# A vision-transformer layer with a routed feed-forward on one core: routing weights spread by DMA, and the instruction orders of four engines rewritten

## The reference, cut to what matters

```python
h = tok(x)                                   # 16 images, 36 patches each: 576 tokens of 192
h = layernorm(h + attn(h))                   # 12 heads of 64, softmax over 36 keys
logits = h @ Wr + br                         # 8 experts
vals, idx = top_k(logits, 2); score = softmax(vals)
gu = h @ Wgu[e] + bgu[e]                     # for every expert e: 2 x 192 columns
gate = min(gu[:192], 7); up = clip(gu[192:], -7, 7)
down_e = ((up + 1) * gate * sigmoid(1.702 * gate)) @ Wd[e] + bd[e]
h = layernorm(h + sum over the 2 chosen e of score[e] * down_e)
```

## Time and profile before

| | us |
|---|---|
| median of 3 runs | 144.47 (144.03 to 145.9) |
| time of the profiled execution | 144.63 |
| its span, first to last instruction | 142.8 |
| PE busy | 132.8 (93%) |
| DVE busy | 101.1 (71%) |
| POOL busy | 79.5 (56%) |
| ACT busy | 76.0 (53%) |
| DMA queue q1, share of its 16 engines | 25.7% |

### The profile page before, as it was taken

How to read it: one execution, slowest core, us unless ns; L and a number is a source line. 1 busy time by engine, 2 the same in 40 slices (tenths; PEclk the granted TensorE clock), 3 DMA queues, 4 the chain that set the end, 5 groups by cost and what they waited for, 6 DMA issues and landing times. The chain is left out here.

```text
span 142.8 us, 4023 instructions
## 1 busy us (share of the span) xinstructions
PE 132.8 (93%) x1586; PEld 123.6 (87%) x1586; DVE 101.1 (71%) x255; ACT 76.0 (53%) x146; POOL 79.5 (56%) x92
## 2 busy tenths in 40 slices
PE   6999999999999999899999993999999999999950
PEld 2779899998989889899899973999999989999940
DVE  0129589468779598656786895478899786788752
ACT  3057889988933564868544481162422455433621
POOL 7303159670499999998640779166353254334511
PEclk9999999999999999999999997799999999999998
DMA  5999955720121225225810000000000000000021
GB/s 134 328 397 409 398 138 134 220 86 0 35 70 46 83 67 152 62 79 146 313 37 0 0 0 7 0 0 0 0 0 5 0 0 0 7 0 2 0 70 54
DMA packets 5962, 12.42 MB, mean 87 GB/s; under 512 B 888, under 2 KB 2872, under 8 KB 5944
## 3 DMA queue, kind: packets, MB, share of 16 engines
q1 hardware_dynamic: 5944, 12.18, 25.7%
HBM read 9.96 MB, written 0.44 MB: 73 GB/s over the span
## 5 line engine op out<-in xcount | busy, mean ns | idle before, releaser
L482 POOL TENSOR_TENSOR reg_r<-reg_p,reg_r 128x324 fp32r<-128x324 f32 (+1 forms) x23 | 19.0, 829 | 21.9 <-ACT reg_r L712 21.9
L408 POOL TENSOR_TENSOR reg_w<-stage,reg_w 128x768 fp32r<-128x768 f32 x12 | 22.5, 1887 | 6.8 <-ACT reg_w L544 6.7
L712 ACT ACTIVATE reg_r<-reg_p 128x324 fp32r<-128x324 f32 (+1 forms) x24 | 10.7, 444 | 27.6 <-DVE reg_p L1061 27.6
L1061 DVE SCALAR_TENSOR_TENSOR reg_p<-reg_q 128x324 f32<-128x324 f32 (+1 forms) x24 | 15.5, 645 | 2.2
L1038 DVE TENSOR_SCALAR reg_q<-ps,bup 128x324 f32<-128x324 f32 (+1 forms) x24 | 12.3, 511 | 6.7 <-PE ps L1283 6.5
L1279 PE MATMUL ps<-reg_r,reg_w 128*128 128x324 f32 (+1 forms) x48 | 15.1, 315 | 0.0
L1280 PE MATMUL ps<-reg_r,reg_w 128*128 128x324 f32 (+1 forms) x48 | 14.5, 302 | 0.0
L1281 PE MATMUL ps<-reg_r,reg_w 128*128 128x324 f32 (+1 forms) x48 | 14.5, 302 | 0.0
L1282 PE MATMUL ps<-reg_r,reg_w 128*128 128x324 f32 (+1 forms) x48 | 14.4, 300 | 0.0
L1283 PE MATMUL ps<-reg_r,reg_w 128*128 128x324 f32 (+1 forms) x48 | 14.3, 299 | 0.0
L703 ACT ACTIVATE reg_q<-ps,sm 128x324 f32<-128x324 f32 (+1 forms) x24 | 11.7, 489 | 3.3 <-PE ps L1283 3.3
(11 more groups left out here) (196 smaller groups left out, 393.5 us busy)
## 6 DMA issues: line engine op xcount, KB each, us to landing
reg_x<-xw_in SPq DMA_DIRECT2D x5, 416.0 KB, 6.1
stage<-w_gu_a SPq DMA_DIRECT2D x4, 384.0 KB, 4.5
stage<-w_gu_b SPq DMA_DIRECT2D x4, 384.0 KB, 3.4
reg_r<-reg_x SPq DMA_DIRECT2D x24, 54.0 KB
stage<-w_qkv_a SPq DMA_DIRECT2D x3, 384.0 KB, 7.7
stage<-w_qkv_b SPq DMA_DIRECT2D x3, 384.0 KB, 8.2
stage<-w_down SPq DMA_DIRECT2D x3, 384.0 KB, 4.0
wout<-w_out SPq DMA_DIRECT2D x1, 576.0 KB, 10.0
```

What stands on the lines that cost most here:

```text
L408: nc.gpsimd.tensor_tensor(dst[:, 1, :], raw, f(dst[:, 0, :]), ALU.subtract).then_inc(s_wlop, 1)
L482: nc.gpsimd.tensor_tensor(acts[:, n % NACT, 1, 0:w], act_f[:, n % 4, 0:w], f(acts[:, n % NACT, 0, 0:w]), ALU.subtract).then_inc(s_alo, 1)
L1061: nc.vector.scalar_tensor_tensor(out=act_f[:, n % 4, 0:w], in0=glu[:, n % 4, 0:w], scalar=GLU_LIMIT, in1=upw[:, n % 4, 0:w], op0=ALU.min, ...
```

## The change

- `spread(n)` leaves PE, and with it the one-hot matrix (and the small POOL and DVE instructions that build it). `choose` now sums its two picks and repeats the eight columns sixteen times, so that after `w_transpose` row p holds the score of expert p mod 8. A new ACT step `w_rows(b)` copies this to SBUF as wrow.
- SP issues 16 DMAs for each half that copy, for every unit, the row of its expert onto the unit's rows. They go from SBUF to SBUF, into the space of xs and V for the first half and into the stage buffers for the second. `weigh(n)` waits for these and reads its score from SBUF, no longer from PSUM.
- The lists of POOL, ACT, DVE and PE are reordered, as the diff shows.

Semaphore lists and the host's layout of bd are left out of the diff.

```diff
@@ -155,6 +154,9 @@
 
+        spread0 = reg_x[:, 0:NT * TS[0]].rearrange("p (c n) -> p c n", c=NT)
+        spread1 = stage[:, :, :].rearrange("p g n -> p (g n)")[:, 0:NT * TS[1]].rearrange("p (c n) -> p c n", c=NT)
+
@@ -350,6 +353,26 @@
                     sp.dma_start(wout[:, :, :], w_out).then_inc(s_wo, 16)
+            def spread(b):
+
+                sp.wait_ge(s_wrow, b + 1)
+                if b == 0:
+                    sp.wait_ge(s_pv, NU)
+                else:
+                    sp.wait_ge(*lo_done(16))
+                dst, cols = (spread0, spread1)[b], slice(TO[b], TO[b] + TS[b])
+
+                def rows(e, c, p0, n):
+                    src = wrow[p0 + e:p0 + n:E, cols].unsqueeze(1).to_broadcast([n // E, E, TS[b]])
+                    sp.dma_start(dst[p0:p0 + n, c, :], src).then_inc(s_spr[NT * b + c], 16)
+
+                for s in range(NPAIR):
+                    rows(2 * s, 3 * s, 0, 128)
+                    rows(2 * s + 1, 3 * s + 1, 0, 128)
+                    rows(2 * s, 3 * s + 2, 0, 64)
+                    rows(2 * s + 1, 3 * s + 2, 64, 64)
+            spread(0)
+            spread(1)
@@ -419,9 +442,6 @@
             nc.gpsimd.tensor_copy(pairs[:, ST:LANES], ident[:, SEQ:64]).then_inc(s_const, 1)
-            nc.gpsimd.tensor_tensor(rows2[:, :], ident[:, 0:2 * E], ident[:, 32:32 + 2 * E], ALU.add).then_inc(s_rows, 1)
-            pool.wait_ge(s_rows, 1)
-            nc.gpsimd.tensor_tensor(rows1[:, :], rows2[:, 0:E], rows2[:, E:2 * E], ALU.add).then_inc(s_rows, 1)
@@ -486,24 +506,25 @@
             for k in range(0, NU):
-                if k in (5, 6):
-                    root(k - 5, TSIZES[k - 5], s_ve, s_rstd)
-                if k in (3, 4, 5, 6):
-                    w_lo((7, 8, 9, 11)[k - 3])
+                if k in (3, 4, 5):
+                    w_lo(k + 4)
+                if k == 6:
+                    w_lo(10)
                 probs(k)
...
                     k_norm(k + 3)
-                if k == 5:
-                    w_lo(10)
+                if k in (4, 5):
+                    root(k - 4, TSIZES[k - 4], s_ve, s_rstd)
             root(2, TSIZES[2], s_ve, s_rstd)
+            w_lo(11)
+            gap_exp(0)
             w_lo(12)
-            gap_exp(0)
             gap_exp(1)
             gap_exp(2)
-            root(3, TSIZES[3], s_ve, s_rstd)
             w_lo(13)
...
             w_lo(15)
+            root(3, TSIZES[3], s_ve, s_rstd)
             act_lo(0)
@@ -512,9 +533,9 @@
             w_lo_tail(16)
+            gap_exp(3)
             act_lo(5)
             act_lo(6)
-            gap_exp(3)
             gap_exp(4)
@@ -685,6 +706,13 @@
                                      ACT.Copy).then_inc(s_h1hi, 1)
+
+            def w_rows(b):
+
+                first, last = W_BATCH[b][0], W_BATCH[b][-1]
+                o, n = TOFFS[first], TOFFS[last] + TSIZES[last] - TOFFS[first]
+                act.wait_ge(s_wt, last + 1)
+                nc.scalar.activation(wrow[:, o:o + n], ps[:, wt_bank(b), 0:n], ACT.Copy).then_inc(s_wrow, 1)
 
@@ -759,24 +787,25 @@
             pt_evac(7)
+            w_hi(13)
+            w_hi(14)
             o_evac(7)
             expert(0)
-            w_hi(13)
+            w_hi(15)
             expert(1)
+            w_hi(16)
+            w_rows(0)
             w2_hi(0)
...
             expert(3)
-            w_hi(14)
-            w_hi(15)
-            w_hi(16)
             act_hi(0)
...
             act_hi(3)
+            h1_evac(4)
             expert(5)
-            h1_evac(4)
             act_hi(4)
@@ -792,7 +821,8 @@
                 act_hi(n if n >= NT + 4 else n - 1)
-                if n == 11:
+                if n == 9:
+                    w_rows(1)
                     w2_hi(1)
@@ -817,9 +847,6 @@
             nc.vector.memset(tiny[:, :], TINY)
-            dve.wait_ge(s_rows, 2)
-            nc.vector.tensor_copy(onehot[:, :].rearrange("p (e n) -> p e n", e=E),
-                                  rows1[:, :].unsqueeze(2).to_broadcast([128, E, 128])).then_inc(s_onehot, 1)
@@ -1010,23 +1037,28 @@
                 rg = rt[:, g % 2]
-                iota = sm[0:n, C_IOTA:C_IOTA + 8].unsqueeze(1).to_broadcast([n, 3, 8])
+                iota = sm[0:n, C_IOTA:C_IOTA + 8]
                 dve.wait_ge(s_idx, g + 1)
                 dve.wait_ge(s_p2, g + 1)
+                if g >= 1:
+                    dve.wait_ge(s_w2, g)
+                for j in range(2):
+                    nc.vector.tensor_scalar(pick[0:n, j, :], iota, rg[0:n, j:j + 1], rg[0:n, 4 + j:5 + j],
+                                            ALU.is_equal, ALU.mult).then_inc(s_w1, 1)
+                dve.wait_ge(s_w1, 2 * g + 2)
                 if g >= 3:
                     dve.wait_ge(s_wt, g - 2)
-                for j in range(2):
-                    nc.vector.tensor_scalar(w2[0:n, g % 3, 0:96].rearrange("p (a e) -> p a e", a=3)[:, :, 8 * j:8 * j + 8],
-                                            iota, rg[0:n, j:j + 1], rg[0:n, 4 + j:5 + j], ALU.is_equal, ALU.mult)\
-                        .then_inc(s_w2, 1)
+                nc.vector.tensor_tensor(w2[0:n, g % 3, :].rearrange("p (a e) -> p a e", e=E),
+                                        pick[0:n, 0:1, :].to_broadcast([n, 16, E]), pick[0:n, 1:2, :].to_broadcast([n, 16, E]),
+                                        ALU.add).then_inc(s_w2, 1)
...
                 dve.wait_ge(s_w2hi, b + 1)
-                nc.vector.tensor_tensor(w2T[32:48, o:o + n], ps[32:48, wt_bank(b), 0:n],
-                                        f(w2T[32:48, o:o + n]), ALU.subtract).then_inc(s_w2lo, 1)
+                nc.vector.tensor_tensor(w2T[32:40, o:o + n], ps[32:40, wt_bank(b), 0:n],
+                                        f(w2T[32:40, o:o + n]), ALU.subtract).then_inc(s_w2lo, 1)
@@ -1040,11 +1072,12 @@
 
-                dve.wait_ge(s_bm, n + 1)
+                a, c = divmod(n, NT)
+                dve.wait_ge(s_spr[n], 32 if c % 3 == 2 else 16)
                 dve.wait_ge(s_u, n + 1)
-                w = TS[n // NT]
+                w = TS[a]
                 nc.vector.scalar_tensor_tensor(out=upw[:, n % 4, 0:w], in0=upw[:, n % 4, 0:w], scalar=1.0 - LIMIT,
-                                               in1=ps[:, B_BANK, 0:w], op0=ALU.max, op1=ALU.mult).then_inc(s_b, 1)
+                                               in1=(spread0, spread1)[a][:, c, :], op0=ALU.max, op1=ALU.mult).then_inc(s_b, 1)
 
@@ -1132,11 +1165,9 @@
             for k in range(2, NU):
-                if k in (5, 6):
-                    ln1_stats(k - 5)
-                row_sum(k)
                 if k == 5:
                     ln1(0)
+                row_sum(k)
                 if k + 1 < NU:
@@ -1144,6 +1175,8 @@
                     q_norm(k + 3)
+                if k in (4, 5):
+                    ln1_stats(k - 4)
             h1_lo(0)
@@ -1165,11 +1198,11 @@
             w2_lo(0)
+            up_in(2)
             ln1(3)
-            up_in(2)
+            h1_lo(3)
             weigh(0)
             expert_act(0)
-            h1_lo(3)
             weigh(1)
@@ -1181,24 +1214,26 @@
             up_in(5)
+            h1_lo(4)
             weigh(4)
             expert_act(4)
-            h1_lo(4)
+            read_logits(3)
+            rank(3)
             up_in(6)
...
             expert_act(5)
+            read_logits(4)
+            router_weights(3)
+            choose(3)
             up_in(7)
...
             expert_act(6)
-            read_logits(3)
-            rank(3)
-            read_logits(4)
+            rank(4)
             up_in(8)
...
             expert_act(7)
-            router_weights(3)
-            choose(3)
-            rank(4)
+            router_weights(4)
+            choose(4)
             for n in range(9, 2 * NT):
@@ -1209,10 +1244,7 @@
                     expert_in(n)
-                if n == 9:
-                    router_weights(4)
-                    choose(4)
-                if n == 11:
+                if n == 10:
                     w2_lo(1)
@@ -1512,26 +1544,6 @@
 
-            def spread(n):
-
-                a, c = divmod(n, NT)
-                s, k = divmod(c, 3)
-                if n == 0:
-                    pe.wait_ge(s_onehot, 1)
-                    pe.wait_ge(s_oev, NU)
-                    pe.wait_ge(s_w2lo, 1)
-                else:
-                    pe.wait_ge(s_b, n)
-                if n == NT:
-                    pe.wait_ge(s_w2lo, 2)
-                first = 256 * s + (0, 128, 64)[k]
-                mm(ps[:, B_BANK, 0:TS[a]], onehot[:, first:first + 128], w2T[:, TO[a]:TO[a] + TS[a]], start=True, stop=True)\
-                    .then_inc(s_bm, 1)
@@ -1599,10 +1611,10 @@
                     v_proj(4, (k - 2,))
+                if k in (4, 5):
+                    project(k - 4)
                 weighted(k - 2)
                 p_transpose(k - 1)
-                if k in (4, 5):
-                    project(k - 4)
             subtract_max(7)
@@ -1621,44 +1633,32 @@
             gate_up(2)
```

(27 more changed lines are left out.)

22 lines of the change are left out of this document (9 added, 13 removed).

## The result

The changed kernel takes 163.2 us (median of 4 runs, 162.12 to 165.48), the kernel before 145.17 beside it: a ratio of 1.1225, 95% interval 1.1084 to 1.1367. It is 12% slower, where I had forecast 3%. The profiled execution lasted 162.42 us, with a span of 160.6.

The account below looks back on a forecast made before the run. It took PE's matmuls to set the pace through the expert stage. Terms: -6.9 + 2.95 + 1.5 + 1.8 + 1.35 + 2.2 + 1.0 = +3.9, on 144.63 giving 148.5 us; range 143.0 to 151.5.

Parts of the forecast that it names:

- the part on h1_transpose(3): Before h1_transpose(3): three w_lo now precede root(3) on POOL, so PE stands 1.5 us (1.2 to 1.8).
- The spreads, -3.1: On PE: removing 24 spread matmuls, 12 x 0.143 + 12 x 0.115, takes 3.1 us off.
- The rest is work: Expert stage on PE: the old order loses about 3.7 us at down(0), and the rest is work.
- down(0), -2.47 and -1.3: At down(0): PE's stand of 2.47 us and 1.3 us of slow matmuls behind it go, 3.8 us gained.
- Attention, +2.95: In attention: PE stands at project(1) and exps(6) starts late on ACT, so project(2) loses 2.95 us (1.4 to 3.3).
- h1_transpose(4), +1.8: Now behind gate_up(4): PE stands 1.6 to 2.1 us for ln1(4), taken as 1.8.
- logits(3), +1.35: Now behind gate_up(5): PE waits 1.35 us (1.1 to 1.5) for h1_lo(4), which stands behind up_in(5) on DVE.
- w_transpose(1), +2.2: Now behind gate_up(9): PE waits for choose(4) on DVE, 1.9 to 3.0 us, taken as 2.2.
- weigh from SBUF, +1.0 for the tail: Second half on DVE: weigh with two SBUF inputs waits for POOL's act_lo; last unit ends 1.0 us late (0 to 3).
- The DMAs, 0: Score copies issued by SP: cost nothing; up to 0.8 us if the stand before weigh(0) weren't there.
- The clock: TensorE's lower level after PE's stands: left out of the sum; each stand like that at down(0) costs up to 1.3 us.
- a stand like the first: The old 2.47 us stand at down(0), followed by the lower clock; each new stand like it costs up to 1.3 us.

Follow-up runs that it names:

- the kernel with the holes alone: Kernel before, products kept; w_hi(14), w_hi(15) moved behind expert(1) on ACT, w_lo(13) ahead of root(3) on POOL after group 2's picks: 140.29 us, ratio 0.9666.
- the kernel with the DMA scores alone: Changed kernel with the instruction lists of POOL, ACT, DVE and PE of the kernel before, each w_rows ahead of its w2_hi: 147.56 us, ratio 1.0108.

## Why the prediction was wrong

The sign and most steps held, the time didn't: 163.2 against 148.5, outside 143.0 to 151.5. Point by point.

- **The step that failed** is in the part on h1_transpose(3): "POOL now does w_lo(13), (14), (15) before root(3)". I followed the three splits on POOL, to root(3), and took DVE's router steps and w_transpose(0) to arrive as before ("unit 0's scores land some 3.2 us after w_transpose(0)" counts from its old time). What they run beside on DVE wasn't asked. The cast waited 5.79 us for them, PE 5.66 at w_transpose(0), a stand that my sum had at nothing. Undoing it gives back 5.3 us. I had the rule for it in hand, in the part on weigh, and applied it to weigh alone. Since DVE was held, root(3) was no longer late, and the 1.5 us forecast there didn't come.
- **The spreads, -3.1:** they gained nothing; with the DMAs the kernel is 1.1% slower. "The rest is work" was the error: PE's 17.00 of 17 shows that PE never waited, not that it alone set the pace. DVE's 15.07 of 17 stood beside it, and I had read it, but only as a limit on what may be added.
- **down(0), -2.47 and -1.3:** the stand went, as forecast, and in the kernel with the holes alone the gain is measured, 4.3 us for my 3.8.
- **Attention, +2.95:** right, the mechanism row by row and the size too: project(2) is 3.18 us late, with the 0.44 lost ahead of the stage taken off, inside my 1.4 to 3.3. The 1.28 us at subtract_max(7) are a part of these. That undoing it gives back more, 5.0 us (known to 2.5), fits the clock, which my sum left out: it is 0.77 from 65 to 70 us in the profile after, and the last section has the same steps at 1.00.
- **h1_transpose(4), +1.8, and logits(3), +1.35:** measured 1.80 and 1.17.
- **w_transpose(1), +2.2:** the path was right, the stand 3.49 us. weigh (0.97 us) and the picks (1.12 us for two) ran under act_lo in that stretch. Those are the terms that I had at their undisturbed price.
- **weigh from SBUF, +1.0 for the tail:** from gate_up(16) to the end the shift against the kernel before grows from 16.2 to 17.8 us, 1.6. The Trainium skill, "SBUF — State Buffer", section "SBUF: two separate sides", gives the exclusive lock; the runs agree for weigh (448 ns from PSUM, 681 and 574 from SBUF).
- **The DMAs, 0:** right in the changed kernel. With the old order weigh(0) waits 0.58 us for its score, within my "up to 0.8 us if the stand weren't there".
- **The clock** was left out of the sum, though six new stands were counted. That was a choice for the low end, and wrong as one: up to 5.2 us by the estimate above. Nor does the condition hold that I gave, a stand like the first: in the kernel with the DMA scores alone PE stands for 2.41 us at down(0), and the clock is 1.00 from 80 to 108.

The parts nearly close: by the ratios, 5.0 (attention) + 5.3 (splits, less what they gain at down(0)) + 4.6 (router) = 14.9 us, and 1.6 for the DMA scores, 16.5 of 17.8 (0.1225 x 145.17). Each carries its share of the clock. Each was undone alone, and each is known to 2 or 3 us, so that the sum comes out is in part luck. The rest, ACT's earlier w_hi and the places of up_in(2) and h1_lo(3) on DVE among it, was undone in none of them.

## What to carry to other kernels

When a POOL instruction is moved, look not only at who waits for it but at what DVE does beside it, down to the smallest copy: a move into POOL's idle time is only free if DVE isn't on the path then, and a wait on DVE's last step there can make it so. It did for one split; for three it moved the stand to root(3). A PE that is always busy doesn't show that its work is the bound; look at the busy share of the next engine before pricing matmuls that are taken away. And a step that is brought forward in an in-order list costs the wait that opens ahead of it, plus all that used to fill that wait.
